# One layer of a post-norm decoder: the rank searches of four heads side by side, selections ahead of them, context in eight parts

## The chip, the cores and the metric

The kernel runs on one core of one Trainium2 chip, as one launch. The metric is device time in microseconds. The kernel before was timed three times: median 5632.22 us (5630.01 to 5635.16). The execution that the profiler recorded is another one, and its own time is 5640.61 us.

## What is computed

A decoder layer over x of shape (4, 1024, 512): windowed self-attention, then a block with cross-attention to a context of shape (4, 2048, 384), then a butterfly feed-forward, each followed by a layer norm. The change touches the cross-attention alone. Of the reference it is this part:

```python
scores = jnp.einsum('bthd,bghd->bhtg', Q, K) / np.sqrt(DH)       # H = 4 heads of 32
scores = jnp.where(vision_mask[:, None, None, :], scores, -jnp.inf)
topv, topi = jax.lax.top_k(scores, K_TOP)                        # 32 of 2048
probs = jax.nn.softmax(topv, axis=-1)
attn = jnp.zeros_like(scores).at[bi, hi, ti, topi].set(probs)
attn_mean = attn.mean(axis=1)                                    # over the heads
c_t = jnp.einsum('btg,bgd->btd', attn_mean, x_vision @ Wv)
```

Every row of every head keeps its 32 largest scores out of 2048; all others get weight zero.

## The kernel before

The layer is a sequence of stages, each with its own buffers and semaphores. `stage_cross` (L1230 to L1641) does the part above up to the mix of the context rows with `attn_mean`. It works on 32 tiles of 128 query rows (`TILES`, L32), eight to a batch (`TPB`, L33). The order of the work is written out by hand, one program for each engine, and the engines meet at semaphores; every engine runs its program in order. Buffers that carry one tile to the next are double (index t % 2).

For tile t and head h:

- **SP** (`_(sp)`) loads the keys of a batch (`keys`), the queries of a tile (`queries`), the parts of the context (`context`, L1317: four parts of 512 rows for a batch through two buffers `raw`, so that parts 2 and 3 wait for `s_clo`), and stores the mixed rows (`store`).
- **PE** computes `scores(t, h)` (L1400: 4 matmuls of 128x512) into `ps_s`, which holds one head: it waits until the head before was copied (`s_sc`). `sum_flags` (L1407) adds the flags of all rows. `turn(t, half, h)` (L1419: 8 matmuls, 16 records) multiplies the selected weights with a diagonal of 1/denominator, so that they come out transposed and summed over the heads. `mix(t)` (L80 to L82: 48 matmuls of 128x384, in three products of high and low parts) multiplies that with the context.
- **ACT** copies scores to `s_buf` (`copy`, L1469), computes the denominators from the 32 tops (`denominators`, L1474), the exponentials of all 2048 scores (`exponentials`, L1480), the high part and a full copy of the turned weights (`hi`, L1487 and L1490), the mixed rows (`mixed`, L1496) and the high part of the context (`context_hi`, L1502).
- **POOL** computes the low parts: `lo` (L1367) of the turned weights, `context_lo` (L1372) of the context.
- **DVE** does the rest. `scan(t, h)` (L1550): 32 MAX8, one for each segment of 64 scores, write 8 ranks of each segment to `cand`. `rank(t, h)` (L1552 to L1571) then finds the 32nd largest: a MAX8 over the low ranks (L1555), four MAX8 over 104 candidates (L1559) with a match_replace between them (L1562, two instructions: the load of the eight values, and the replacement), and a scalar_tensor_tensor with an accumulator that counts candidates at or above the 32nd (L1568, two instructions too). Each reads what the one before wrote, so a `dve.drain()` stands behind each. `settle(t)` (L1573) loads the four flag sums into registers and branches: a head whose sum shows a possible miss is searched over all 2048 scores. `diagonals` (L1602, L1607) and `select(t, h)` (L1596: keep the exponential where the score is at least the 32nd largest) follow.

The order on DVE in iteration t, which does the selections of tile t and the searches of tile t + 1: 8 segments of head 0, the copy of the flag sums (L1616), 8 segments, `settle(t)`, 16 segments, `rank` 0, `diagonals`, `select` 0 and 1, `scan` and `rank` 1, `select` 2 and 3, `scan` and `rank` 2, `scan` and `rank` 3, then L1639 (`nmax`: the negated row maxima) and the semaphore `s_cand`. `sum_flags(t + 1)` on PE waits for `s_cand`, and L1616 of the next iteration for `sum_flags`. `denominators(t)` on ACT waits for `s_chk`, which `settle(t)` gives.

The order on PE in iteration t: `sum_flags(t)`, `mix(t-1)`, `scores(t+1, 2)`, `turn(t, 0, 0..1)`, `scores(t+1, 3)`, `turn(t, 0, 2..3)`, `turn(t, 1, 0)`, `scores(t+2, 0)`, `turn(t, 1, 1..3)`, `scores(t+2, 1)`.

## Time and profile before

| what | value |
|---|---|
| median of 3 runs | 5632.22 us |
| the profiled execution's own time | 5640.61 us |
| its span, first to last instruction | 5638.9 us |
| TensorE clock granted, mean of the span (1.0 is 2.4 GHz) | 0.860 |
| cross-attention stage, in the span | about 1449 to 3059 us |
| PE, DVE, ACT, POOL busy in the whole span | 73%, 56%, 24%, 28% |

Durations below come from the profiled execution. In a timeline the columns are: start in us from the span's start, length in us of the group of instructions on the row, engine, line, operation, out<-in and shapes, number of records (a float32 matmul of `turn` leaves two records), and in brackets the idle time of the engine just before with what ended it. The length of a row with several instructions runs from the first start to the last end.

### The profile page before, as it was taken

The numbers are of one execution on the slowest core, as the hardware profiler recorded it, in microseconds if no ns is written. First come the engines' busy times: TensorE is split into PE (matmuls) and PEld (weight loads), VectorE is DVE, ScalarE is ACT, GpSimd is POOL, SyncE is SP. The second block draws the span as 40 slices with busy tenths as digits, with TensorE's granted clock in tenths as the row PEclk, the third lists the DMA queues.
The fourth block names the chain that finished last, engine by engine and source line by source line (L and its number), as shares of the span: only waits on it lengthen the run. The fifth ranks groups of instructions, "written<-read, shape, count | busy, mean of one in ns | idle before, by whom it ended". The sixth has DMA issues, their size and how long they took to land. (4 is left out here: it accounts for less than half of the span.)

```text
span 5638.9 us, 66043 instructions
## 1 busy us (share of the span) xinstructions
PE 4120.7 (73%) x20932; PEld 3402.2 (60%) x20932; DVE 3146.1 (56%) x9382; ACT 1364.4 (24%) x2042; POOL 1596.3 (28%) x1280
## 2 busy tenths in 40 slices
PE   2331239997467677565676996869699999499998
PEld 1331127775366666465665685657588888388887
DVE  8959933443588888988884454542323433322222
ACT  1210112332344444343442000012211111211111
POOL 2537200000111211110210461320266766133332
PEclk8555669998688888787888998989799999799999
DMA  0025131223301001001000342333412211200000
GB/s 10 17 68 209 45 86 53 82 81 112 121 9 43 21 10 43 17 10 43 21 8 37 117 144 97 112 121 112 128 60 68 76 58 49 90 19 25 20 24 21
DMA packets 238144, 350.47 MB, mean 62 GB/s; under 512 B 67090, under 2 KB 117138, under 8 KB 234002
## 3 DMA queue, kind: packets, MB, share of 16 engines
q1 hardware_dynamic: 145444, 187.77, 10.9%
q10 hardware_dynamic: 89856, 151.04, 7.8%
q0 software_dynamic: 2560, 8.39, 0.4%
q8 instruction: 115, 1.88, 0.1%
q14 instruction: 169, 1.38, 0.1%
HBM read 240.13 MB, written 107.00 MB: 62 GB/s over the span
## 5 line engine op out<-in xcount | busy, mean ns | idle before, releaser
L1419 PE MATMUL xa_ps_t<-xa_diag,xa_s_buf 128*128 128x128 f32 x4096 | 604.0, 316 | 403.8 <-DVE xa_s_buf L1596 331.9
L1419 PEld LDWEIGHTS xa_ps_t<-xa_diag,xa_s_buf 128*128 128x128 f32 x4096 | 581.4, 229 | 442.5 <-DVE xa_s_buf L1596 362.3
L2746 DVE CAST m_act_hl<-m_g 128x512 fp32r<-128x512 f32 x256 | 138.1, 539 | 892.9 <-ACT m_g L2634 892.9
L1550 DVE MAX8 xa_cand<-xa_s_buf 128x8 f32<-128x64 f32 x4096 | 538.6, 216 | 110.9 <-issue 83.3
L2495 POOL TENSOR_TENSOR m_act_hl<-m_g,m_act_hl 128x512 fp32r<-128x512 f32 x256 | 352.7, 1378 | 701.3 <-DVE m_act_hl L2746 701.3
L1367 POOL TENSOR_TENSOR xa_aT<-xa_a,xa_aT 128x512 fp32r<-128x512 f32 x128 | 160.7, 1276 | 1198.5 <-ACT xa_a L1490 1198.5
L2634 ACT ACTIVATE m_g<-m_ps_h,m_b 128x512 f32<-128x512 f32 x256 | 176.1, 688 | 1103.2 <-PE m_ps_h L82 1103.2
L80 PE MATMUL m_ps_h<-m_hT,m_w 128*128 128x512 f32 x1024 | 412.2, 403 | 12.3 <-DVE m_w L2725 7.6
L82 PE MATMUL m_ps_h<-m_hT,m_w 128*128 128x512 f32 x1024 | 404.6, 395 | 0.0
L81 PE MATMUL m_ps_o<-m_w,m_act_hl 128*128 128x512 f32 x1024 | 404.4, 395 | 0.0
L82 PE MATMUL m_ps_o<-m_w,m_act_hl 128*128 128x512 f32 x1024 | 404.4, 395 | 0.0
L81 PE MATMUL m_ps_h<-m_hT,m_w 128*128 128x512 f32 x1024 | 404.3, 395 | 0.0
L80 PE MATMUL m_ps_o<-m_w,m_act_hl 128*128 128x512 f32 x1024 | 404.1, 395 | 0.0
L1469 ACT ACTIVATE xa_s_buf<-xa_ps_s 128x2048 f32<-128x2048 f32 x128 | 241.3, 1885 | 336.1 <-PE xa_ps_s L1400 336.1
L1596 DVE SCALAR_TENSOR_TENSOR xa_s_buf<-xa_s_buf,xa_top,xa_prob 128x2048 f32<-128x2048 f32 x128 | 307.9, 2448 | 6.8 <-ACT xa_prob L1480 0.8
L1480 ACT ACTIVATE xa_prob<-xa_s_buf,xa_nmax 128x2048 f32<-128x2048 f32 x128 | 252.0, 1993 | 15.6 <-DVE xa_s_buf L1596 15.6
L80 PE MATMUL xa_ps_ac<-xa_ctx_hl,xa_aT 128*128 128x384 f32 x512 | 198.8, 388 | 57.0 <-POOL xa_aT L1367 57.0
L80 PEld LDWEIGHTS m_ps_h<-m_hT,m_w 128*128 128x128 f32 x1024 | 193.7, 189 | 60.7 <-issue 10.7
L82 PEld LDWEIGHTS m_ps_h<-m_hT,m_w 128*128 128x128 f32 x1024 | 193.4, 189 | 45.3
L80 PEld LDWEIGHTS m_ps_o<-m_w,m_act_hl 128*128 128x128 f32 x1024 | 192.2, 188 | 46.8 <-POOL m_act_hl L2495 1.0
L82 PEld LDWEIGHTS m_ps_o<-m_w,m_act_hl 128*128 128x128 f32 x1024 | 192.0, 188 | 46.4
L81 PEld LDWEIGHTS m_ps_o<-m_w,m_act_hl 128*128 128x128 f32 x1024 | 192.0, 188 | 45.8
(372 smaller groups left out, 8765.2 us busy)
## 6 DMA issues: line engine op xcount, KB each, us to landing
at_xk<-in_x_dram SPq DMA_DIRECT2D x128, 128.0 KB, 2.6
spectrum<-df_yo ACTq DMA_DIRECT2D x32, 512.0 KB, 2.8
id_raw<-spectrum SPq DMA_DIRECT2D x32, 512.0 KB, 3.9
m_xt<-x ACTq DMA_DIRECT2D x64, 256.0 KB, 3.3
bf_w_dn<-_L_ffn_down_weights_dram SPq DMA_DIRECT2D x7, 2048.0 KB, 7.2
bf_w_up<-in_L_ffn_up_weights_dram ACTq DMA_DIRECT2D x7, 2048.0 KB, 10.1
ky_raw<-in_ctx_dram SPq DMA_DIRECT2D x16, 768.0 KB, 6.4
xa_ks<-kt SPq DMA_DIRECT2D x48, 256.0 KB
```

The lines of the kernel that those rows point to most:

```text
L80: pe.matmul(out, w_hi, m_lo, start=start, stop=False)
L81: pe.matmul(out, w_lo, m_hi, start=False, stop=False)
L82: return pe.matmul(out, w_hi, m_hi, start=False, stop=stop)
L1367: pool.tensor_tensor(aT[:, 1, 4 * g:4 * g + 4, :], a32[:, g % 2, :, :], aT[:, 0, 4 * g:4 * g + 4, :].bitcast(F32), ALU.subtract).then_inc( ...
L1419: last = pe.matmul(ps_t[:, c // 4, c % 4, :], s_buf[:, t % 2, h, k0:k0 + P], diag[:, h, :], start=(h == 0 and c % 4 == 0), stop=(h == HEAD ...
L1469: act.activation(s_buf[:, t % 2, h, :], ps_s[:, :, :].rearrange("p c n -> p (c n)"), ACT.Copy).then_inc(s_sc, 1)
L1480: act.activation(prob[:, h % 2, :], s_buf[:, t % 2, h, :], ACT.Exp, bias=nmax[:, t % 2, h:h + 1], scale=SCALE).then_inc(s_exp, 1)
L1550: dve.max(out=ranks[:, :, g], in_=s_buf[:, t % 2, h, g * SEG:(g + 1) * SEG])
L1596: dve.scalar_tensor_tensor(out=s_buf[:, t % 2, h, :], in0=s_buf[:, t % 2, h, :], scalar=top[:, t % 2, h, TOPK - 1:TOPK], in1=prob[:, h % 2 ...
L2495: pool.tensor_tensor(lo, g32[:, :], hi.bitcast(F32), ALU.subtract).then_inc(s_gl, 1)
L2634: act.activation(g32[:, :], ps_h[:, n % 2, :], ACT.Gelu, bias=b1[:, n:n + 1]).then_inc(s_g, 1)
L2746: dve.tensor_copy(act_hl[:, n % 2, 0, :], g32[:, :]).then_inc(s_gh, 1)
```

## The change

The searches of the four heads of a tile are done together: each of the four heads has its own `cand` and `cand_b`, and every step of `rank` is issued for the four heads in turn, with one drain behind the four. All of it stands at the end of the iteration, behind `scan` 3; `select` 2 and 3 stand ahead of `scan` 3. The flag sums are copied after 16 segments where it was 8, and `settle` comes after all 32. On PE `scores(t+1, 1)` and `scores(t+1, 2)` stand between `sum_flags(t)` and `mix(t-1)`. On ACT and POOL `hi` and `lo` of quarters 2 and 3 of a tile move into the next iteration, on ACT behind `copy(t+1, 1)`. `copy(t+1, 3)` moves behind `exponentials(t, 3)` and `mixed(t-1)`. The context comes in eight parts of 256 rows for a batch, again through two buffers. The output of L1568 that nobody reads goes to `cand_b` as bfloat16, where it went to a buffer of its own.

```diff
 ident = sb("ident", [P, P])
-raw = sb("raw", [P, 2, 4, DV])
+raw = sb("raw", [P, 2, 2, DV])
 ctx_hl = sb("ctx_hl", [P, 2, GC, DV], F32R)
 ...
-cand = sb("cand", [P, 2 * BACK])
-cand_b = sb("cand_b", [P, NW])
+cand = sb("cand", [P, HEADS, 2 * BACK])
+cand_b = sb("cand_b", [P, HEADS, NW])
 top = sb("top", [P, 2, HEADS, TOPK])
-f_junk = sb("f_junk", [P, 2, NW])
 f_weight = sb("f_weight", [P, 2, NW])
 ...
         def context(b, g):
-            i = 4 * b + g
+            i = 8 * b + g
             if i >= 2:
 ...
             sp.dma_start(raw[:, g % 2, :, :],
-                         A["ctx_768"][b][g * 512:(g + 1) * 512, :].rearrange("(n p) v -> p n v", p=P)
+                         A["ctx_768"][b][g * 256:(g + 1) * 256, :].rearrange("(n p) v -> p n v", p=P)
                          ).then_inc(s_raw[g % 2], 16)
 ...
         def store(t):
 ...
             if t % TPB == 0:
-                context(b, 2)
-                context(b, 3)
+                for g in range(2, 8):
+                    context(b, g)
             if t >= 1:
 ...
         def context_lo(b, g):
-            pool.wait_ge(s_chi, 4 * b + g + 1)
-            pool.tensor_tensor(ctx_hl[:, 1, 4 * g:4 * g + 4, :], raw[:, g % 2, :, :],
-                               ctx_hl[:, 0, 4 * g:4 * g + 4, :].bitcast(F32), ALU.subtract).then_inc(s_clo, 1)
+            pool.wait_ge(s_chi, 8 * b + g + 1)
+            pool.tensor_tensor(ctx_hl[:, 1, 2 * g:2 * g + 2, :], raw[:, g % 2, :, :],
+                               ctx_hl[:, 0, 2 * g:2 * g + 2, :].bitcast(F32), ALU.subtract).then_inc(s_clo, 1)
 ...
         for t in range(TILES):
+            if t >= 1:
+                lo(t - 1, 2)
+                lo(t - 1, 3)
             if t % TPB == 0:
-                context_lo(t // TPB, 0)
-                context_lo(t // TPB, 1)
+                for g in range(4):
+                    context_lo(t // TPB, g)
             lo(t, 0)
 ...
             if t % TPB == 0:
-                context_lo(t // TPB, 2)
-                context_lo(t // TPB, 3)
-            lo(t, 2)
-            lo(t, 3)
+                for g in range(4, 8):
+                    context_lo(t // TPB, g)
+        lo(TILES - 1, 2)
+        lo(TILES - 1, 3)
 ...
     def _(pe):
 ...
         def mix(t):
 ...
             if t % TPB == 0:
-                pe.wait_ge(s_clo, 4 * (t // TPB + 1))
+                pe.wait_ge(s_clo, 8 * (t // TPB + 1))
             if t >= 1:
 ...
-        scores(0, 0)
-        scores(0, 1)
-        scores(0, 2)
-        scores(0, 3)
+        for h in range(HEADS):
+            scores(0, h)
         scores(1, 0)
-        scores(1, 1)
         for t in range(TILES):
             sum_flags(t)
+            if t + 1 < TILES:
+                scores(t + 1, 1)
+                scores(t + 1, 2)
             if t >= 1:
                 mix(t - 1)
-            if t + 1 < TILES:
-                scores(t + 1, 2)
             turn(t, 0, 0)
 ...
             turn(t, 0, 3)
-            turn(t, 1, 0)
             if t + 2 < TILES:
                 scores(t + 2, 0)
-            turn(t, 1, 1)
-            turn(t, 1, 2)
-            turn(t, 1, 3)
-            if t + 2 < TILES:
-                scores(t + 2, 1)
+            for h in range(HEADS):
+                turn(t, 1, h)
         mix(TILES - 1)
 ...
         def context_hi(b, g):
-            act.wait_ge(s_raw[g % 2], 16 * (2 * b + g // 2 + 1))
+            act.wait_ge(s_raw[g % 2], 16 * (4 * b + g // 2 + 1))
             if b >= 1:
                 act.wait_ge(s_ac, b * TPB)
-            act.activation(ctx_hl[:, 0, 4 * g:4 * g + 4, :], raw[:, g % 2, :, :], ACT.Copy).then_inc(s_chi, 1)
+            act.activation(ctx_hl[:, 0, 2 * g:2 * g + 2, :], raw[:, g % 2, :, :], ACT.Copy).then_inc(s_chi, 1)
 ...
         for t in range(TILES):
 ...
                 copy(t + 1, 1)
+            if t >= 1:
+                hi(t - 1, 2)
+                hi(t - 1, 3)
             denominators(t)
 ...
             exponentials(t, 2)
-            if t + 1 < TILES:
-                copy(t + 1, 3)
             exponentials(t, 3)
 ...
                 mixed(t - 1)
+            if t + 1 < TILES:
+                copy(t + 1, 3)
             if t % TPB == 0:
-                context_hi(t // TPB, 0)
-                context_hi(t // TPB, 1)
+                for g in range(4):
+                    context_hi(t // TPB, g)
             hi(t, 0)
 ...
             if t % TPB == 0:
-                context_hi(t // TPB, 2)
-                context_hi(t // TPB, 3)
-            hi(t, 2)
-            hi(t, 3)
+                for g in range(4, 8):
+                    context_hi(t // TPB, g)
+        hi(TILES - 1, 2)
+        hi(TILES - 1, 3)
         mixed(TILES - 1)
 ...
     def _(dve):
-        dve.memset(cand[:, :], 0.0)
+        dve.memset(cand[:, :, :], 0.0)
         dve.memset(f_weight[:, 0, :], 1.0)
 ...
         dve.drain()
-        ranks = cand[:, 8:NC].rearrange("p (r g) -> p r g", g=SEGS)
+        ranks = [cand[:, h, 8:NC].rearrange("p (r g) -> p r g", g=SEGS) for h in range(HEADS)]
+        junk = cand_b[:, :, :].rearrange("p h n -> p (h n)").bitcast(BF16).rearrange("p (h a x) -> p h a x", h=HEADS, a=2)
 ...
         def scan(t, h, first, last):
 ...
             for g in range(first, last):
-                dve.max(out=ranks[:, :, g], in_=s_buf[:, t % 2, h, g * SEG:(g + 1) * SEG])
-        def rank(t, h):
+                dve.max(out=ranks[h][:, :, g], in_=s_buf[:, t % 2, h, g * SEG:(g + 1) * SEG])
+        def rank(t):
             k = t % 2
             dve.drain()
-            dve.max(out=cand[:, 0:8], in_=cand[:, NW:NC])
-            dve.drain()
-            src = cand[:, 0:NW]
+            for h in range(HEADS):
+                dve.max(out=cand[:, h, 0:8], in_=cand[:, h, NW:NC])
+            dve.drain()
+            src = cand[:, :, 0:NW]
             for r in range(TOPK // 8):
-                dve.max(out=top[:, k, h, 8 * r:8 * r + 8], in_=src)
+                for h in range(HEADS):
+                    dve.max(out=top[:, k, h, 8 * r:8 * r + 8], in_=src[:, h, :])
                 dve.drain()
                 if r < TOPK // 8 - 1:
-                    dve.match_replace(out=cand_b[:, :], in_to_replace=top[:, k, h, 8 * r:8 * r + 8], in_values=src,
-                                      imm_value=TAKEN)
+                    for h in range(HEADS):
+                        dve.match_replace(out=cand_b[:, h, :], in_to_replace=top[:, k, h, 8 * r:8 * r + 8],
+                                          in_values=src[:, h, :], imm_value=TAKEN)
                     dve.drain()
-                src = cand_b[:, :]
-            dve.scalar_tensor_tensor(out=f_junk[:, :, :], in0=cand[:, :].rearrange("p (a x) -> p a x", a=2)[:, :, 0:NW],
-                                     scalar=top[:, k, h, TOPK - 1:TOPK], in1=f_weight[:, :, :],
-                                     op0=ALU.is_ge, op1=ALU.mult, accum_out=flag[:, k, h:h + 1])
-            dve.drain()
+                src = cand_b[:, :, :]
+            for h in range(HEADS):
+                dve.scalar_tensor_tensor(out=junk[:, h, :, :],
+                                         in0=cand[:, h, :].rearrange("p (a x) -> p a x", a=2)[:, :, 0:NW],
+                                         scalar=top[:, k, h, TOPK - 1:TOPK], in1=f_weight[:, :, :],
+                                         op0=ALU.is_ge, op1=ALU.mult, accum_out=flag[:, k, h:h + 1])
+            dve.tensor_scalar(nmax[:, k, :], top[:, k, :, 0], -SCALE, None, ALU.mult)
+            dve.drain().then_inc(s_cand, 1)
 ...
         def settle(t):
 ...
             if more:
-                scan(t + 1, 0, 0, 8)
+                scan(t + 1, 0, 0, 16)
             if t >= 0:
 ...
             if more:
-                scan(t + 1, 0, 8, 16)
+                scan(t + 1, 0, 16, SEGS)
             if t >= 0:
 ...
             if more:
-                scan(t + 1, 0, 16, SEGS)
-                rank(t + 1, 0)
+                scan(t + 1, 1, 0, SEGS)
             if t >= 0:
 ...
             if more:
-                scan(t + 1, 1, 0, SEGS)
-                rank(t + 1, 1)
+                scan(t + 1, 2, 0, SEGS)
             if t >= 0:
 ...
             if more:
-                for h in range(2, HEADS):
-                    scan(t + 1, h, 0, SEGS)
-                    rank(t + 1, h)
-                dve.tensor_scalar(nmax[:, (t + 1) % 2, :], top[:, (t + 1) % 2, :, 0], -SCALE, None, ALU.mult)
-                dve.drain().then_inc(s_cand, 1)
+                scan(t + 1, 3, 0, SEGS)
+                rank(t + 1)
 st.clear()
 ...
```

## Rows read from the trace of the kernel before

**Rows 1.** Window from first to last L1639: us, busy of PE, PEld, DVE, ACT, POOL; clock

```profile
1500.00:3012.00 1512.00, 1010.97 (x5958) 945.82 (x5958) 1311.98 (x5964) 664.17 (x788) 221.87 (x140) 0.83 0.08 22
```

**Rows 2.** Groups of DVE instructions by line, 1440 to 3065 us: busy, mean ns | idle before

```profile
L1550 DVE MAX8 xa_cand<-xa_s_buf 128x8 f32<-128x64 f32 x4096 | 538.6, 216 | 110.9 <-issue 83.3 <-ACT xa_s_buf L1469 19.2
...
L1596 DVE SCALAR_TENSOR_TENSOR xa_s_buf<-xa_s_buf,xa_top,xa_prob 128x2048 f32<-128x2048 f32 x128 | 307.9, 2448 | 6.8 <-ACT xa_prob L1480 0.8
...
L1568 DVE SCALAR_TENSOR_TENSOR xa_f_junk<-xa_cand,xa_top,xa_f_weight 128x208 f32<-128x208 f32 x128 | 71.5, 559 | 9.9 <-issue 0.4
...
L1639 DVE TENSOR_SCALAR xa_nmax<-xa_top 128x4 f32<-128x4 f32 x32 | 28.5, 892 | 2.6
```

**Rows 3.** Timeline of DVE, one head's scan and rank, up to the next scan

```profile
1955.18 4.15 DVE L1550 MAX8 xa_cand<-xa_s_buf 128x8 f32<-128x64 f32 x32
1959.41 0.33 DVE L1555 MAX8 xa_cand<-xa_cand 128x8 f32<-128x160 f32 x1
1959.81 0.27 DVE L1559 MAX8 xa_top<-xa_cand 128x8 f32<-128x104 f32 x1
1960.15 0.09 DVE L1562 MATCH_VALUE_LOAD xa_cand_b<-xa_top,xa_cand 128x8 f32 x1
1960.23 0.25 DVE L1562 MATCH_REPLACE8 xa_cand_b<-xa_top,xa_cand 128x104 f32<-128x104 f32 x1
1960.56 0.27 DVE L1559 MAX8 xa_top<-xa_cand_b 128x8 f32<-128x104 f32 x1
...
1962.39 0.43 DVE L1568 SCALAR_TENSOR_TENSOR xa_f_junk<-xa_cand,xa_top,xa_f_weight 128x208 f32<-128x208 f32 x1
1962.76 0.08 DVE L1568 DVE_READ_ACCUMULATOR xa_f_junk<-xa_cand,xa_top,xa_f_weight 128x1 f32 x1
1962.91 4.16 DVE L1550 MAX8 xa_cand<-xa_s_buf 128x8 f32<-128x64 f32 x32
```

**Rows 4.** Timeline of DVE, one whole tile, from one L1639 to the next

```profile
2017.08 0.17 DVE L1639 TENSOR_SCALAR xa_nmax<-xa_top 128x4 f32<-128x4 f32 x1
...
2022.73 2.13 DVE L1550 MAX8 xa_cand<-xa_s_buf 128x8 f32<-128x64 f32 x16 [2.77 <-issue]
...
2028.43 0.18 DVE L1602 RECIPROCAL xa_rec<-xa_den 128x4 f32<-128x4 f32 x1
...
2029.68 4.62 DVE L1596 SCALAR_TENSOR_TENSOR xa_s_buf<-xa_s_buf,xa_top,xa_prob 128x2048 f32<-128x2048 f32 x2
...
2061.97 0.17 DVE L1639 TENSOR_SCALAR xa_nmax<-xa_top 128x4 f32<-128x4 f32 x1
```

**Rows 5.** Timelines of ACT: the copy of head 3 before tile 0, a `hi`

```profile
1479.33 1.88 ACT L1469 ACTIVATE xa_s_buf<-xa_ps_s 128x2048 f32<-128x2048 f32 x1 [2.23 <-PE xa_ps_s L1400]
...
2017.57 0.60 ACT L1487 ACTIVATE xa_aT<-xa_ps_t 128x512 fp32r<-128x512 f32 x1 [3.48 <-PE xa_ps_t L1419]
```

**Rows 6.** Timeline of POOL, the two `lo` that `mix` waits for

```profile
2018.73 2.49 POOL L1367 TENSOR_TENSOR xa_aT<-xa_a,xa_aT 128x512 fp32r<-128x512 f32 x2 [9.70 <-ACT xa_a L1490]
```

**Rows 7.** Timelines of PE: `scores` at either clock, `turn` at either clock

```profile
1500.22 2.08 PE L1400 MATMUL xa_ps_s<-xa_ks,xa_qs 128*128 128x512 f32 x4
...
2007.59 3.65 PE L1419 MATMUL xa_ps_t<-xa_diag,xa_s_buf 128*128 128x128 f32 x16 [2.25 <-ACT xa_a L1490]
...
2031.27 1.09 PE L1400 MATMUL xa_ps_s<-xa_ks,xa_qs 128*128 128x512 f32 x4
...
2055.26 5.52 PE L1419 MATMUL xa_ps_t<-xa_diag,xa_s_buf 128*128 128x128 f32 x48
```

**Rows 8.** The context: instructions on `xa_raw` (ns min/median/max), DMA issues (us to landing)

```profile
L1502 ACT ACTIVATE xa_ctx_hl<-xa_raw x16: 1472/1476/1482, 1525.8 to 2731.1; 128x1536 fp32r<-128x1536 f32 x16
L1372 POOL TENSOR_TENSOR xa_ctx_hl<-xa_raw,xa_ctx_hl x16: 3469/3562/5498, 1527.4 to 2734.7; 128x1536 fp32r<-128x1536 f32 x16
...
xa_raw<-in_ctx_dram SPq DMA_DIRECT2D x16, 768.0 KB, 5.6
...
m_xt<-w SPq DMA_DIRECT2D x32, 256.0 KB, 3.5
```

## The prediction, made before the changed kernel ran

> **What bounds the kernel now.** The busy shares of the page come first: over the whole span no engine is above 73%, so a stage has to be chosen. The window of the tile loop [rows 1] is that choice: from the first L1639 to the last are 1512 us for 31 tiles, 48.8 us a tile. DVE is busy for 1312 of them, PE for 1011 at a granted clock of 0.83, ACT for 664. The waits view gives DVE almost nothing but "issue" waits, that is, no other engine keeps it (the largest are the 83.3 us ahead of L1550 [rows 2], one gap a tile). So DVE's own instruction stream sets the time. The timeline of one tile [rows 4] shows it whole: 44.89 us from one L1639 to the next, one gap of 2.77 us (the four flag sums go into registers and `settle` branches), all else back to back. That is a clean tile. The others are longer for two reasons. Heads are searched again in full in two tiles, which stays. And three kinds of DVE instruction are at times stretched [rows 2]: L1639 takes 892 ns in the mean against 170 undisturbed [rows 4], L1568 559 against 430 [rows 3], L1596 2448 against about 2350 (the pair in [rows 4] less its overlap). My reading of the timelines is that this happens where a POOL tensor_tensor runs beside them, as `lo` does behind L1639 [rows 6]. Together: 32 x 0.72 + 128 x 0.13 + 128 x 0.10 = 52 us.
>
> **Part 1, the searches side by side.** One head costs 7.72 us from scan to scan [rows 3]: 4.23 us to the first instruction of `rank`, 3.50 us for `rank`. In `rank` each instruction is followed by a drain, start to start: L1555 0.40 us, L1559 0.34, the L1562 pair 0.41, the L1568 pair 0.52. What does an instruction cost when the next one belongs to another head and needs no drain? 32 scans run in 4.15 us and last 0.216 each [rows 2, 3], so they start every (4.15 - 0.216) / 31 = 0.127 us: each starts 0.09 before its predecessor ends. The accumulator read starts 0.37 after L1568, which lasts 0.43: an overlap of 0.06 to 0.07 between two instructions of different kinds. I price accordingly:
> - L1555: 3 x (0.33 - 0.09) + 0.40 = 1.12 us for four heads.
> - L1559, four rounds: 4 x (3 x 0.18 + 0.34) = 3.52.
> - L1562, three rounds: the load takes 0.08 to the replacement, which gives 0.18 after its overlap with the next head's load (the nearest row is the accumulator read's, of another kind too): 3 x (3 x 0.26 + 0.41) = 3.57. Bounds: 0.24 with 0.09 of overlap, 0.34 with none, so 3.4 to 4.3.
> - L1568: 3 x 0.44 + 0.52 = 1.84.
>
> Sum 10.05 against 4 x 3.50 = 14.0: 3.95 saved. Three scans also lose the drain behind them and flow on: 3 x (4.23 - 32 x 0.127) = 0.5. So 4.45 us a tile, 31 tiles: **-138 us**. The bfloat16 target of L1568 changes nothing: its two inputs stay float32. I take it at zero.
>
> The rule against this part is in the Trainium skill, VectorE: DVE Perf Modes, The DRAIN you can't avoid: after every Vector instruction the pipe empties before the next starts, chaining does not help, only fewer instructions do. By it the change would save explicit drains alone; the starts of the scans every 0.127 us speak against it here.
>
> **Part 2, the first search** (before tile 0) saves less. The copies come every 4.1 us whatever DVE does; the copy of head 3 ends at 1481.2 [rows 5]. Then 4.23 + 10.05 + 0.3 gives 1495.8, where the loop now begins at about 1500.1 (the first row of [rows 7] starts there): **-4.3**.
>
> **Part 3, a clean tile laid out anew.** Let D be the end of L1639 with its drain; all in us after D. DVE: 32 scans of head 0 with the flag copy between them 4.3, register gap 2.8: 7.1. Scan 1: 11.2. Diagonals 1.25 [rows 4]: 12.5. Two selects 4.53 (2029.68 to 2034.21): 17.0. Scan 2: 21.1. Selects 2 and 3: 25.6. Scan 3 29.8, `rank` 39.9, L1639 40.2. (44.89 - 4.45 gives 40.4.) The gap could shrink by the eight more scans that now stand between flag copy and loads, 1.0 us a tile or -31 us, if they queue up behind the loads; or not at all. The nearest row is the gap itself, with eight scans ahead of it, so I take no gain and keep -31 for the range.
>
> Do the others keep up?
> - PE: `sum_flags`, then `scores(t+1, 1)`, with the copy 2.1 behind its start at half clock [rows 7]. ACT: copy until 4.1, `hi` 2 and 3 until 6.0. POOL's `lo` start 1.16 after their `hi` and take 2.5 [rows 5, 6]: 7.7. Only then can `mix(t-1)` start; now it starts at about 1. Its length: 2018.73 + 2.49 to 2031.27 [rows 6, 7], 10.05 us: it ends at 17.8. This is the new wait of the change, and behind it on PE stand all turns and `scores(t+1, 3)`.
> - Turns 0 and 1, 5.27 / 3 = 1.76 each at full clock [rows 7]: 21.3. `scores(t+1, 3)` 22.4, its copy by ACT 1.9: 24.4. DVE wants it at 25.6. **Slack 1.2 us, the smallest in the tile.**
> - Turns 2 and 3 wait for selects: 27.4; `scores(t+2, 0)` 28.5; `hi` 0 and 1: 29.6; four turns: 36.6. The flags are asked for at 40.2. Slack 3.6.
> - ACT has the exponentials of heads 0, 1, 2, 3 by 10.5, 12.5, 17 and 19, each before its select. `copy(t+1, 2)` by 14.4.
>
> So in a clean tile no wait shows, and the moved steps cost nothing as long as this holds.
>
> **Part 4, POOL beside DVE.** `lo` 2 and 3 now run at 5.2 to 7.7, beside scans and the gap; `lo` 0 and 1 at 29 to 31.3, beside scan 3 and the first MAX8 of `rank`. None of the three kinds that are stretched is near. Of the 52 us I keep 4 for context tiles: **-48**.
>
> **Part 5, the context** (4 tiles). Half a part costs 0.74 on ACT and 1.78 on POOL [rows 8]; its load, between 3.5 us (256 KB) and 5.6 (768 KB) for 384 KB: 4.0. Two buffers hold two parts, but ACT now wants four in a row. Parts 0 and 1 are copied by 25.9; part 2 can load only after POOL has done part 0 (27.0) and lands at 31.0, part 3 at 32.8; `hi` 0 and 1 end at 35.5, turns of half 1 begin 6 late after 7 us of idle, so the first at half clock (3.65 [rows 7]): done at 44.7. The flag copy wants PE at 42.5: 2.3 lost. Parts 6 and 7 again wait for loads, ACT is free at 50.0, `copy(t+2, 1)` ends at 51.9 where DVE wants it at 49.9: 2.0 lost. `mix` starts late at 55.6, and with it the copy for scan 3 comes 1.9 late. Sum 6.2 x 4: **+25 us**. Bounds: 0 (each load inside its cover) to 12 a tile, +48.
>
> **Sum** against the profiled execution: 5640.6 - 138 - 4.3 - 48 + 25 = 5475. The median of the runs was 8.4 us under it: **5467 us**.
>
> **Rivals.**
> - *No overlap between heads*: the next instruction starts only when the last has ended. Each instruction gives only its drain: 3 x 0.09 + 12 x 0.09 + 9 x 0.08 + 3 x 0.07 = 2.3 us less a tile, 32 times: 5467 + 73 = 5540. For it: L1562's load may have to wait until the replacement is done with its eight values. Against: the scans. 10%. It is also what the rule of the Trainium skill named in part 1 would give.
> - *The copy for scan 3 is late.* The slack of 1.2 us goes if `mix` ramps up longer or the two turns behind it run at half clock (3.5 more). At 1 to 2 us a tile, 31 to 62 us: 5498 to 5529. For it: every stall in the chain above adds up here. 17%.
> - *The same part, more of it*, with 3 to 5 us a tile: 5560 to 5620. 6%.
> - *Slower than before*: PE becomes the bound at 1.2 GHz. It idles three times ahead of `mix`, and gaps of that size are followed by half clock now (the row of [rows 7] with 2.25 before it). Its work from 7.7 on is mix 10.05 + turns 14.1 + scores 2.2 = 26.3 us; if all of it takes twice as long, PE ends at 63 and not 36.6, and a tile takes about 60 us: 31 x 20 more, 6080. It decides from the point where PE's work takes 9 us more (45.7 a tile, the 165 us given back), a third more than reckoned. Against: from `mix` to the last turn PE is idle for hardly 2 us. 4%.
> - *The change does not do what it says* (another thing than the stream of DVE sets the time, and nothing moves): [rows 4] leave no room. 2%.
>
> **How the numbers follow.** The forecast, 5435 to 5498, has 61%. The range takes in the early register loads (-31), the dearer L1562 (+25), the dearer context, the late copy and the case of no overlap: 5435 to 5545. The bound for "same" is 0.2%, 11 us, about what a measurement can tell. Faster has all of the forecast and the first three rivals: 0.93; same 0.02; slower 0.05.
>
> **What would show it.** In the changed profile: L1639 to L1639 in 40.4 us; L1559 starting every 0.18 us within four; L1562 pairs every 0.26; L1639 at 0.17 us always; `mix` starting 7.7 us after L1639; no wait of DVE on an ACT copy except behind context tiles. DVE waiting for `xa_s_buf` in every tile would make it wrong; so would L1562 at 0.34 or PE waited for by the flag copy.

## The result, and the profile after

The changed kernel takes 5427.84 us in the median of 4 runs (5423.54 to 5428.57), the kernel before 5631.78 us (four runs, where the table ahead of the prediction has three): a ratio of 0.9636 (95% interval 0.9619 to 0.9652), 204 us faster. The forecast was 5467 us, with a range from 5435 to 5545. The direction was right; the gain was larger than the range allowed, by 7 us at its low end.

The profiled executions are 217 us apart (5640.61 and 5423.54 us). Where that lies is read from the rows of L1639 before and of L1576 after, which are the same instruction (it writes `nmax` and ends the search). The timeline of DVE, first and last of the 32, with the first scan of the stage; first the kernel before:

```profile
1468.92 4.16 DVE L1550 MAX8 xa_cand<-xa_s_buf 128x8 f32<-128x64 f32 x32 [19.25 <-ACT xa_s_buf L1469]
...
1499.84 0.17 DVE L1639 TENSOR_SCALAR xa_nmax<-xa_top 128x4 f32<-128x4 f32 x1
...
3011.78 1.05 DVE L1639 TENSOR_SCALAR xa_nmax<-xa_top 128x4 f32<-128x4 f32 x1
```

and the changed kernel:

```profile
1461.17 16.47 DVE L1550 MAX8 xa_cand<-xa_s_buf 128x8 f32<-128x64 f32 x128 [17.89 <-ACT xa_s_buf L1465]
1486.95 0.17 DVE L1576 TENSOR_SCALAR xa_nmax<-xa_top 128x4 f32<-128x4 f32 x1
...
2796.22 0.16 DVE L1576 TENSOR_SCALAR xa_nmax<-xa_top 128x4 f32<-128x4 f32 x1
```

| stretch, us | before | after | difference | forecast |
|---|---|---|---|---|
| up to the first scan (see below) | 1468.92 | 1461.17 | -7.8 | 0 |
| first search | 30.92 | 25.78 | -5.1 | -4.3 |
| 31 tiles | 1511.9 | 1309.3 | -202.7 | -161 |
| from there to the end | 2627.1 | 2625.7 | -1.4 | 0 |

Nearly all of it is the loop. The 7.8 us ahead of the first scan are no effect that the runs show: of what stands there the change touches one memset (0.33 us before, 1.12 after) and the size of the context's loads, which are issued behind the keys; and in the traces of the ten variants below, which share the changed kernel's opening, the first scan starts anywhere from 1461.4 to 1469.0 us. A clean tile takes 38.71 us (of the 31 intervals, 17 lie between 38.6 and 38.8) where it took 44.89 [rows 4] and was forecast at 40.4. This is one, in the timeline of DVE of the changed kernel:

```profile
2010.29 0.17 DVE L1576 TENSOR_SCALAR xa_nmax<-xa_top 128x4 f32<-128x4 f32 x1
2010.57 2.13 DVE L1550 MAX8 xa_cand<-xa_s_buf 128x8 f32<-128x64 f32 x16
2012.61 0.13 DVE L1622 CAST xa_flag_i<-xa_ps_f 1x4 int32<-1x4 f32 x1
2012.82 2.13 DVE L1550 MAX8 xa_cand<-xa_s_buf 128x8 f32<-128x64 f32 x16
2017.13 4.15 DVE L1550 MAX8 xa_cand<-xa_s_buf 128x8 f32<-128x64 f32 x32 [2.18 <-issue]
2021.20 0.16 DVE L1608 RECIPROCAL xa_rec<-xa_den 128x4 f32<-128x4 f32 x1
...
2035.55 4.15 DVE L1550 MAX8 xa_cand<-xa_s_buf 128x8 f32<-128x64 f32 x32
2039.77 1.01 DVE L1556 MAX8 xa_cand<-xa_cand 128x8 f32<-128x160 f32 x4
2040.85 0.77 DVE L1561 MAX8 xa_top<-xa_cand 128x8 f32<-128x104 f32 x4
2041.70 0.09 DVE L1565 MATCH_VALUE_LOAD xa_cand_b<-xa_top,xa_cand 128x8 f32 x1
2041.78 0.25 DVE L1565 MATCH_REPLACE8 xa_cand_b<-xa_top,xa_cand 128x104 f32<-128x104 f32 x1
2041.94 0.08 DVE L1565 MATCH_VALUE_LOAD xa_cand_b<-xa_top,xa_cand 128x8 f32 x1
...
2048.28 0.43 DVE L1572 SCALAR_TENSOR_TENSOR xa_cand_b<-xa_cand,xa_top,xa_f_weight 128x208 bf16<-128x208 f32 x1
2048.64 0.09 DVE L1572 DVE_READ_ACCUMULATOR xa_cand_b<-xa_cand,xa_top,xa_f_weight 128x1 f32 x1
2048.64 0.43 DVE L1572 SCALAR_TENSOR_TENSOR xa_cand_b<-xa_cand,xa_top,xa_f_weight 128x208 bf16<-128x208 f32 x1
...
2048.99 0.17 DVE L1576 TENSOR_SCALAR xa_nmax<-xa_top 128x4 f32<-128x4 f32 x1
```

Four heads' searches take from 2039.77 to 2048.99, 9.22 us, where one took 3.50 [rows 3]. The replacement that lasts 0.25 is followed by the next head's value load 0.16 after its start. The accumulator read and the next head's L1572 start at the same time, so a pair costs 0.36. Behind the fourth L1572 L1576 follows at the same pace: this last step has no drain between its instructions and L1576, though the change is described above as one drain behind every step of four. The register gap is 2.18 us where it was 2.77. Apart from that gap there is no wait.

The groups of DVE (columns as in [rows 2]) show the other half of the gain: nothing is stretched any more, but for L1572, which is at 450 against an undisturbed 430.

```profile
L1602 DVE SCALAR_TENSOR_TENSOR xa_s_buf<-xa_s_buf,xa_top,xa_prob 128x2048 f32<-128x2048 f32 x128 | 294.7, 2345 | 4.4 <-ACT xa_prob L1476 0.8
...
L1572 DVE SCALAR_TENSOR_TENSOR xa_cand_b<-xa_cand,xa_top,xa_f_weight 128x208 bf16<-128x208 f32 x128 | 50.5, 450 | 2.4
...
L1576 DVE TENSOR_SCALAR xa_nmax<-xa_top 128x4 f32<-128x4 f32 x32 | 5.3, 166 | 0.0
```

Record by record the traces tie this to POOL. Of the 32 L1639 of the kernel before, the 21 that a POOL instruction overlaps in time take 1270 ns in the mean, the other 11 take 170. Of the 128 L1568 it is 34 at 904 ns against 94 at 434, of the 128 L1596 8 at 3942 against 120 at 2348. The MAX8 of the scans take 216 ns either way. What these three kinds take above their undisturbed length sums to 52 us in the loop of the kernel before and to 3 us in that of the changed one.

Of these 3 us 2 lie in the last interval, which is longer by 2.4 (41.11 us). There is no next tile, so ACT and POOL come to quarters 2 and 3 early, and two of the last four L1572 run beside POOL and take 1.43 and 1.42 us. DVE first, then POOL, in the timelines of the changed kernel:

```profile
2793.50 1.43 DVE L1572 SCALAR_TENSOR_TENSOR xa_cand_b<-xa_cand,xa_top,xa_f_weight 128x208 bf16<-128x208 f32 x1
...
2794.86 1.42 DVE L1572 SCALAR_TENSOR_TENSOR xa_cand_b<-xa_cand,xa_top,xa_f_weight 128x208 bf16<-128x208 f32 x1
...
2793.42 2.63 POOL L1366 TENSOR_TENSOR xa_aT<-xa_a,xa_aT 128x512 fp32r<-128x512 f32 x2 [7.13 <-ACT xa_a L1486]
```

The first of them starts 0.08 us after POOL's first instruction and ends at 2794.93; the second starts 0.07 us before that and ends at 2796.28, when POOL's second has ended at 2796.05. The Trainium skill says of this (SBUF — State Buffer, SBUF: two separate sides) that VectorE and GpSimd share a pair of ports as an exclusive lock, which whoever starts first keeps for the whole instruction, and that a two-port mode or two SBUF inputs are enough to need it. These rows agree: 1.43 where 0.43 is undisturbed, and MAX8, with one input, is not stretched beside POOL. L1639 has only one tensor input and is stretched all the same; whether it runs in such a mode, no row here shows.

Against that stands the context. Around a context tile two intervals together take 9 to 10 us more than two clean ones (38.99 + 48.53 around tile 8). The waits of DVE from 1840 to 1900 us (who waited for whom: us in total, times, longest):

```profile
DVE xa_cand L1550 <- ACT xa_s_buf L1465: 9.1, 3, 4.0
DVE xa_flag_i L1622 <- PE xa_ps_f L1409: 2.5, 1, 2.5
```

### The profile page after: what moved, and what is told of

It is laid out like the page before. It is cut to its first block and busy times, and to the rows that moved or that the text cites. A ratio compares the mean times of both kernels' runs of the same rounds, so it can differ in the third digit from the quotient of the medians.

```text
span 5421.9 us, 65111 instructions
## 1 busy us (share of the span) xinstructions
PE 4071.0 (75%) x20932; PEld 3333.7 (61%) x20932; DVE 2998.4 (55%) x9382; ACT 1368.5 (25%) x2058; POOL 1589.7 (29%) x1296
## 5 line engine op out<-in xcount | busy, mean ns | idle before, releaser
L1421 PE MATMUL xa_ps_t<-xa_diag,xa_s_buf 128*128 128x128 f32 x4096 | 504.5, 284 | 164.6 <-DVE xa_s_buf L1602 98.4
L1421 PEld LDWEIGHTS xa_ps_t<-xa_diag,xa_s_buf 128*128 128x128 f32 x4096 | 487.3, 198 | 196.1 <-DVE xa_s_buf L1602 117.1
L1602 DVE SCALAR_TENSOR_TENSOR xa_s_buf<-xa_s_buf,xa_top,xa_prob 128x2048 f32<-128x2048 f32 x128 | 294.7, 2345 | 4.4 <-ACT xa_prob L1476 0.8
L1402 PE MATMUL xa_ps_s<-xa_ks,xa_qs 128*128 128x512 f32 x512 | 188.7, 501 | 107.1 <-ACT xa_s_buf L1465 85.1
L80 PEld LDWEIGHTS m_ps_o<-m_w,m_act_hl 128*128 128x128 f32 x1024 | 192.5, 188 | 46.6 <-POOL m_act_hl L2496 1.1
L82 PEld LDWEIGHTS m_ps_o<-m_w,m_act_hl 128*128 128x128 f32 x1024 | 192.4, 188 | 46.2
## 6 DMA issues: line engine op xcount, KB each, us to landing
bf_w_up<-in_L_ffn_up_weights_dram ACTq DMA_DIRECT2D x7, 2048.0 KB, 10.1
```

Of the source, the lines that this page charges most:

```text
L80: pe.matmul(out, w_hi, m_lo, start=start, stop=False)
L82: return pe.matmul(out, w_hi, m_hi, start=False, stop=stop)
L1402: last = pe.matmul(ps_s[:, c, :], qs[:, t % 2, h, :], ks[:, h, c * 512:(c + 1) * 512], start=True, stop=True)
L1421: last = pe.matmul(ps_t[:, c // 4, c % 4, :], s_buf[:, t % 2, h, k0:k0 + P], diag[:, h, :], start=(h == 0 and c % 4 == 0), stop=(h == HEAD ...
L1602: dve.scalar_tensor_tensor(out=s_buf[:, t % 2, h, :], in0=s_buf[:, t % 2, h, :], scalar=top[:, t % 2, h, TOPK - 1:TOPK], in1=prob[:, h % 2 ...
```

## The experiments

Ten kernels ran, each timed against the kernel before on the same chip. The kernel before took 5633.64 us on the chip of the first four, 5628.60 on that of the next four and 5638.01 on that of the last two, so a difference of a few us between two kernels is read from their traces and not from the medians. "Tile" is the most frequent interval between two of the `nmax` instructions, read from the timeline.

**A drain behind every instruction of the search.** Order and heads stay as in the changed kernel:

```diff
 for h in range(HEADS):
     dve.max(out=cand[:, h, 0:8], in_=cand[:, h, NW:NC])
-dve.drain()
+    dve.drain()
```

and likewise behind L1561, L1565 and L1572.

> The changed kernel with a drain behind every instruction of the rank search, order kept. Theory (the overlap of one head's instruction with the next one's is what pays): a rank step costs again what it cost alone, 4 x 0.40 + 16 x 0.34 + 12 x 0.41 + 4 x 0.52 = 14.0 us for four heads against 9.2 in the changed kernel, the clean tile goes from 38.7 to 43.5 us, the kernel to 5428 + 32 x 4.8 = 5582 us. Rival (only the 27 drains themselves cost, 0.08 us each, nothing overlaps): tile 40.9 us, kernel 5495 us.

Measured: 5569.95 us, ratio 0.9888 (0.9872 to 0.9905); tiles of 43.5 to 44.4 us. The edit adds 28 drains a tile and not 27, since the step of L1572 had none. The search takes 2196.55 to 2210.56 = 14.0 us again, and each L1572 pair 0.52:

```profile
2208.99 0.44 DVE L1572 SCALAR_TENSOR_TENSOR xa_cand_b<-xa_cand,xa_top,xa_f_weight 128x208 bf16<-128x208 f32 x1
2209.36 0.08 DVE L1572 DVE_READ_ACCUMULATOR xa_cand_b<-xa_cand,xa_top,xa_f_weight 128x1 f32 x1
2209.51 0.43 DVE L1572 SCALAR_TENSOR_TENSOR xa_cand_b<-xa_cand,xa_top,xa_f_weight 128x208 bf16<-128x208 f32 x1
```

So 142 of the 204 us hang on the instructions of different heads running into one another without a drain. The order alone brings nothing in the search. That the kernel came out 12 us under the 5582 has a cause outside the search: in the longer tile the other engines have more slack, and the context tiles cost 14 us over clean ones where they cost 38 in the changed kernel. The rival is out: it forecast 5495. The Trainium skill (VectorE: DVE Perf Modes, The DRAIN you can't avoid) says that the next instruction does not start until the pipe is empty, and in the same paragraph that one which is not held starts earlier. The prediction took only the first sentence from it. The changed kernel's rows agree with the second: without a drain the starts come 0.07 to 0.09 us before the predecessor's end, for the replacement and the accumulator's instruction too.

**`hi` and `lo` of quarters 2 and 3 back in their own iteration** (ACT and POOL; the same edit in both):

```diff
-                    if t >= 1:
-                        lo(t - 1, 2)
-                        lo(t - 1, 3)
...
+                    lo(t, 2)
+                    lo(t, 3)
```

> The changed kernel with hi and lo of quarters 2 and 3 back in their own iteration, on ACT and POOL alone. Theory (POOL beside L1572 and L1576 stretches them): lo then runs at about 38 to 40.5 us after the last L1576, just where L1572 and L1576 of the search stand; their means rise by some 0.3 us and more, a tile takes 1 to 2 us more, the kernel 5460 to 5490 us. Rival (the place of lo does not matter): 5428 us, L1572 at 0.43 and L1576 at 0.17 us.

Measured: 5454.27 us, ratio 0.968 (0.9664 to 0.9696). Tiles of 38.7, 39.8 and 40.8 us side by side. The groups show where it went:

```profile
L1566 DVE SCALAR_TENSOR_TENSOR xa_cand_b<-xa_cand,xa_top,xa_f_weight 128x208 bf16<-128x208 f32 x128 | 66.1, 571 | 2.4
...
L1570 DVE TENSOR_SCALAR xa_nmax<-xa_top 128x4 f32<-128x4 f32 x32 | 17.8, 556 | 0.0
```

571 and 556 ns where the changed kernel has 450 and 166 (line numbers are six lower here). 128 x 0.12 + 32 x 0.39 + 128 x 0.02 for the selections = 31 us; the medians differ by 26. The theory holds, at 6 us under its band. As in the kernel before, the stretched records are those that POOL overlaps: the 35 such L1566 take 944 ns in the mean, the other 93 take 431; the 12 such L1570 take 1215, the other 20 take 161. Intervals are 38.7 as in the changed kernel, or longer by 1.1 or 2.1 us, according to which instructions meet POOL.

**The flag copy after 24, and after 8, of the 32 segments** (two kernels):

```diff
-                        scan(t + 1, 0, 0, 16)
+                        scan(t + 1, 0, 0, 24)
...
-                        scan(t + 1, 0, 16, SEGS)
+                        scan(t + 1, 0, 24, SEGS)
```

> The changed kernel with the flag copy after 24 segments, so 8 scans stand between it and the register loads, as in the kernel before. Theory (the gap is the 3.6 us from the first load to the next scan, less the scans already queued; the loads start once about ten scans are still to run): gap 2.8 us and not 2.2, tile 39.3, kernel 5446 us. Rival (the gap does not depend on it): 5428 us.

> The changed kernel with the flag copy after 8 segments, so 24 scans stand between it and the register loads. Theory (a queue takes only about ten scans ahead of the loads): gap 2.2 us as with 16, tile 38.7, kernel 5428 us. Rival (all scans run ahead of the loads, eight more hide 1.0 us more): gap 1.2 us, tile 37.7, kernel 5397 us.

Measured: 5445.16 us (0.9666, 0.965 to 0.9683), tile 39.3, and 5427.85 us (0.9636, 0.962 to 0.9652), tile 38.7. The next scan in either, from the timelines:

```profile
2066.95 4.16 DVE L1550 MAX8 xa_cand<-xa_s_buf 128x8 f32<-128x64 f32 x32 [2.76 <-issue]
```

```profile
2059.98 4.16 DVE L1550 MAX8 xa_cand<-xa_s_buf 128x8 f32<-128x64 f32 x32 [2.17 <-issue]
```

With eight scans behind the flag copy the gap is 2.76 us, with 16 it is 2.18, with 24 it stays 2.17. The rows of the register loads say why: the first starts 0.2 us after the scans resume with 8 behind, 0.6 with 16, 1.7 with 24. With 16 and with 24 that leaves 11 scans still to start in most tiles (9 in a few). DVE's sequencer gets that far ahead and no farther. From the first load to the next scan are 3.7 us in most tiles of all three (four loads with the tests of their bounds, then four branches), so about 1.5 us can be hidden behind scans, the rest not. The Trainium skill gives VectorE a queue of eight (Advanced Engine Details and Errata, Engine Queue Depths); what is measured here is that and mostly three more.

**DVE's part and the context's alone**, with the orders of PE, ACT and POOL as before:

```diff
-                    if t + 1 < TILES:
-                        scores(t + 1, 1)
-                        scores(t + 1, 2)
                     if t >= 1:
                         mix(t - 1)
+                    if t + 1 < TILES:
+                        scores(t + 1, 2)
...
+                    if t + 2 < TILES:
+                        scores(t + 2, 1)
```

(and `hi`, `lo`, `turn(t, 1, 0)` and `copy(t+1, 3)` at their old places).

> The changed kernel with the orders of PE, ACT and POOL as before (hi and lo in their own iteration, scores(t+1, 1) at the end of the iteration before, mix ahead of scores(t+1, 2), copy(t+1, 3) ahead of exponentials(t, 3)); DVE and the eight context parts as changed. Theory: DVE's part gives most, but select 3 waits for its exponential by about 0.5 us, and lo stretches L1572 and L1576: tile about 41 us, kernel 5480 to 5520 us. Rival (the other engines' orders do not matter): 5428 us.

Measured: 5511.80 us, ratio 0.9793 (0.9773 to 0.9813), tile 41.0 us. The size was right, the reason was not. L1569, which is L1572 of the changed kernel, is at 432 ns, undisturbed: in that order the search falls between POOL's instructions (in the tile below POOL works until 2040.80 and again from 2050.48, L1569 runs from 2045.86 to 2047.36). The tile is longer by waits of scan 2 for its copy and of the flag copy for PE:

```profile
2050.38 0.15 DVE L1619 CAST xa_flag_i<-xa_ps_f 1x4 int32<-1x4 f32 x1 [0.68 <-PE xa_ps_f L1406]
...
2066.14 4.16 DVE L1547 MAX8 xa_cand<-xa_s_buf 128x8 f32<-128x64 f32 x32 [1.30 <-ACT xa_s_buf L1465]
```

Scan 2 starts 18.57 us after the tile's first scan (2047.57), where the changed kernel has 16.41 (2010.57 to 2026.98): these two waits are nearly all of the 2.3 us. So of the 204 us about 120 come with the other engines in their old order (the context's eight parts apart); their new order is worth the other 84. Both waits end at PE: the flag sums stand behind `scores(t+2, 1)`, and `scores(t+1, 2)` behind `mix`. No run changed PE's order alone. Context tiles suffer most here (53 to 54 us): they make 14 of the 84.

**The context's parts spread over four places; then with three buffers as well:**

```diff
                     if t % TPB == 0:
-                        for g in range(4):
-                            context_hi(t // TPB, g)
+                        context_hi(t // TPB, 0)
+                        context_hi(t // TPB, 1)
                     hi(t, 0)
                     hi(t, 1)
+                    if t % TPB == 0:
+                        context_hi(t // TPB, 2)
+                        context_hi(t // TPB, 3)
```

with parts 4 and 5 behind `copy(t+2, 0)`, and 6 and 7 behind `hi(t, 3)` in the next iteration; POOL likewise. For three buffers: `raw` is `[P, 3, 2, DV]`, a part goes to buffer i % 3 and waits for `s_clo >= i - 2`.

> The changed kernel with the eight context parts taken two by two at four places (ahead of hi 0 and 1, behind them, behind copy(t+2, 0), behind hi 2 and 3 of the next iteration) where it took four in a row twice. Theory (a third part in a row waits on ACT for a load, and DVE waits for ACT's copies): the 9.1 us that a context tile takes more go to 3 to 5 us, kernel 5408 to 5415 us; no wait of ACT for the context's DMA above 1 us. Rival (the work itself, not the wait for the loads, costs the time): 5428 us.

> As the run with the context parts spread, and with three buffers for the parts where it had two. Theory: no load is waited for; a context tile takes 0 to 3 us more than a clean one, kernel 5396 to 5408 us. Rival (the loads were covered already with two): as the spread version.

Measured: 5417.42 us (0.9625, 0.9608 to 0.9643) and 5405.92 us (0.9603, 0.9585 to 0.962). The two intervals around tile 8 take 42.4 + 42.5 us and 40.2 + 41.9, against 39.0 + 48.5: 10.1 us over two clean ones, 7.5 and 4.7. The intervals of the ratios overlap with that of the changed kernel; the loop of 31 tiles in the traces, 1309.3 us in the changed kernel, 1299.8 and 1288.6 in these two, shows the gain. ACT's wait for the context's DMA in the three kernels:

```profile
ACT xa_ctx_hl L1498 <- DMA xa_raw<-in_ctx_dram: 49.4, 16, 5.4
```

```profile
ACT xa_ctx_hl L1501 <- DMA xa_raw<-in_ctx_dram: 18.3, 16, 2.2
```

```profile
ACT xa_ctx_hl L1503 <- DMA xa_raw<-in_ctx_dram: 7.1, 4, 1.9
```

Spreading alone took 10 us off the kernel, not 13 to 20, since waits of 0.6 to 2.2 us for loads were left; and with three buffers one load a batch is still waited for, against the theory. With three buffers the kernel's time is in the band, but a context tile still costs 4.7 and not 0 to 3. Two things remain. In the second interval it is scan 3: `mix` waits for parts 6 and 7, and the copy behind it comes 3.3 us late with two buffers, 2.7 with three (around tile 8). In the first it is POOL again: spread out, `context_lo` now meets the instructions that count candidates (L1583 here), which take 3.1 of the 3.7 us with two buffers and all of the 1.5 with three. DVE, then POOL, with three buffers:

```profile
1845.71 1.96 DVE L1583 SCALAR_TENSOR_TENSOR xa_cand_b<-xa_cand,xa_top,xa_f_weight 128x208 bf16<-128x208 f32 x1
...
1845.64 1.80 POOL L1373 TENSOR_TENSOR xa_ctx_hl<-xa_raw,xa_ctx_hl 128x768 fp32r<-128x768 f32 x1 [0.61 <-ACT xa_ctx_hl L1503]
```

**One register load a tile.** The four flags are also summed, and the single ones are loaded only if the sum shows a doubt:

```diff
                         dve.tensor_copy(flag_i[:, 0:HEADS], ps_f[:, :])
+                        dve.tensor_reduce(out=flag_i[:, HEADS:HEADS + 1], in_=ps_f[:, :], axis=AX.X, op=ALU.add)
...
+                    total = dve.value_load(flag_i[0:1, HEADS:HEADS + 1], min_val=0, max_val=P * NW * 16)
+                    with dve.If(total > HEADS * P * TOPK):
```

> The changed kernel with the sum of the four flags as a fifth value: one register load and one branch a tile, the four others only where it shows a doubt. Theory (the register gap is loads and branches, and the copy for scan 3 has 1.0 us of slack): the gap of 2.2 us goes, but scan 3 then waits about 1.2 us for its copy: tile 37.7, kernel 5397 us. Rival (nothing else binds): tile 36.6, kernel 5363 us.

Measured: 5410.68 us, ratio 0.9612 (0.9594 to 0.963), tile 37.8. The gap has gone (the last 16 scans of head 0 and the 32 of head 1 run on as one group of 48), and scan 3 waits:

```profile
2008.63 6.41 DVE L1550 MAX8 xa_cand<-xa_s_buf 128x8 f32<-128x64 f32 x48
...
2030.42 4.16 DVE L1550 MAX8 xa_cand<-xa_s_buf 128x8 f32<-128x64 f32 x32 [1.05 <-ACT xa_s_buf L1465]
```

2.18 less, 1.05 more make 1.13, of which the tile shows 0.94: the slack of the copy for scan 3 was about 1 us, as reckoned. The kernel gained 17 us (the loop 20, from 1309.3 to 1289.2), not the 31 expected, since some tiles wait longer (39.3 to 39.7) and the contexts no less.

**And `scores(t+1, 3)` directly behind `mix(t-1)`:**

```diff
                         mix(t - 1)
+                    if t + 1 < TILES:
+                        scores(t + 1, 3)
                     turn(t, 0, 0)
                     turn(t, 0, 1)
-                    if t + 1 < TILES:
-                        scores(t + 1, 3)
```

> As the run with one register load, and on PE scores(t+1, 3) directly behind mix(t-1), ahead of the turns of heads 0 and 1. Theory (the 1.05 us for which scan 3 waited in that run is PE's order and nothing else): the copy of head 3 is done 3.5 us earlier, no wait is left in a clean tile, tile 36.7 us, kernel 5411 - 31 x 1.1 = 5377 us. Rival (the turns, now 1.1 us later, make the next flags late or scan 3 waits all the same): tile 37.5 us or more, kernel about 5405 us.

Measured: 5369.73 us, ratio 0.953 (0.9514 to 0.9546), tile 36.7: the wait was PE's order, and the turns behind it hold nobody up in a clean tile. The kernel gained 41 us and not 34, since the tiles that had waited longer than 1.05 us lost that too.

**All of these together** (one load, `scores(t+1, 3)` early, parts spread, three buffers):

> One register load, scores(t+1, 3) behind mix, the context parts spread over four places and three buffers for them. Theory: the gains add up, 5428 - 51 (load and order) - 22 (context) = 5355 us; a context tile 2 to 4 us longer than a clean one of 36.7. Rival (with the shorter tile PE or ACT has no slack left for the context, and the context's gain is lost): about 5377 us.

Measured: 5351.57 us, ratio 0.9496 (0.9481 to 0.9512): 76 us below the changed kernel and the fastest version here. Clean tiles take 36.7, around tile 8 it is 38.6 + 39.0; 1.65 of the 1.9 us in the first of these are again instructions stretched beside POOL. Of the scans' waits in DVE's list this is left:

```profile
DVE xa_cand L1561 <- ACT xa_s_buf L1470: 18.2, 2, 18.0
...
DVE xa_cand L1561 <- issue: 4.3, 9, 1.1
```

18.0 of the first row is the wait for the stage's first copy.

## Why the prediction was right or wrong

**What bounds** was right: DVE's own stream, before and after. No other engine is seen in a clean tile, and the forecast waits (`mix` 7.7 us after the search, 6.8 measured; the copy for scan 3 with 1.2 us of slack, 0.9 measured, 2034.64 against 2035.55) are where they were put.

**Part 1, the searches** is the step that failed: the mechanism was right and the price of four heads side by side, 10.05 us, too dear; 9.22 were measured. The mechanism (0.09 us of overlap for each instruction) is shown by the run with the drains put back. Term by term, for four heads: L1555 1.12 forecast, 1.08 measured; L1559 3.52 and 3.40; L1562 3.57 and 3.33, so the lower bound that was left aside (0.24 a pair) was the right one; L1568 1.84 and 1.42. Of these last 0.42 us, 0.25 are that the next head's instruction starts with the accumulator read and not behind it (3 pairs at 0.36 and not 0.44); the other 0.17 are that the prediction took 0.52 for the fourth pair, a drain included, where the change has none: it takes as long as the others. Sum 10.05 and 9.22: 0.83 x 31 = 26 us. The range had room for a dearer search and hardly any for a cheaper one (0.2 us a tile by the lower bound of L1562, or 6 us): for L1568 no bound was given at all. The -31 us of the range's low end were meant for the register gap. With the search at its forecast price the kernel would have come out at about 5454 us, inside.

**The sum used the smaller of two gains.** The tile laid out anew gave 40.2 us, the difference method 40.4, and the difference was not looked into. A clean tile measured 38.71, 1.73 less than 40.44: 0.83 are the search, 0.59 the gap, 0.31 are left. Of these 0.2 stand in the tile of [rows 4] itself. Its flag copy waited for PE, here in the timelines of DVE and PE before:

```profile
2017.37 1.12 DVE L1550 MAX8 xa_cand<-xa_s_buf 128x8 f32<-128x64 f32 x8
2018.61 0.15 DVE L1616 CAST xa_flag_i<-xa_ps_f 1x4 int32<-1x4 f32 x1
...
2018.38 0.19 PE L1407 MATMUL xa_ps_f<-xa_flag,xa_ones 128*1 128x4 f32 x2
```

The copy starts 0.12 us behind the scans and 0.04 behind PE's flag sums, where it starts 0.09 before the scans' end in the changed kernel (2012.61 against 2012.70). The layout had left this out, the difference carried it on. Counted over 31 tiles the 0.31 are 10 us.

**Part 3, the register gap.** "No gain taken, -31 for the range": 0.59 us a tile of 1.0 came, 18 us. The runs with the flag copy moved show why: the sequencer gets ahead by about eleven scans and no more.

**Part 4, POOL beside DVE** was right in place and size: with 44.89 for each of 31 tiles and 70 us for the repeated searches, before has about 50 us left over, and the stretched instructions sum to 52; after, beside the context's 38, 3 are left, 2.4 of them in the last interval. The run with `lo` put back brought half of it back.

**Part 5, the context** had the mechanism and too small a size: 25 us forecast, 38 measured (the eight intervals around the context tiles against 38.71). Around tile 8 the flags waited 2.5 (2.3 forecast), scan 1 4.0 where 2.0 were forecast beyond the gap (4.0 - 2.2 = 1.8), scan 3 3.0 (1.9 forecast); and scan 0, for which nothing was forecast, waited 2.1: `copy(t+2, 0)` stands behind the four parts too.

Together -26 - 18 - 10 + 13 = -41 of the 42 us by which the loop was missed. The context's 13 us too little hid as much of the other errors; that was luck. Outside the loop, 8 of the 52 us between 5475 and 5423.5 lie ahead of the first scan and are scatter, as the openings of the other runs show. Between the medians the miss is 39 us.

**The rivals.** "No overlap" is ruled out by the starts 0.17 us apart. "The copy is late" did not come, though it was 0.9 us away, and the run with one load shows it as soon as the tile shrinks. PE never fell behind: its last turn ended at 2047.4, 1.9 us ahead of the next flags, less than the 3.6 reckoned because DVE got there sooner (PE was done 36.8 us after the search, 36.6 reckoned).

## What to carry to other kernels

Where short dependent VectorE instructions need a drain each, issue several independent chains in turn: here the same instructions took 9.2 us and not 14.0, and of the 4.8 us only 2.2 were the 28 drains (an estimate, at the 0.08 us between an instruction's end and the next start with a drain between). Keep scalar_tensor_tensor with two SBUF inputs, and small instructions like L1639, away from POOL's tensor_tensor in time; here a place beside the MAX8 scans or the register gap cost nothing. When two ways of summing one forecast differ, find out why before taking the smaller, and bound a price from both sides.

## What was not expected

An accumulator read and the next scalar_tensor_tensor start at the same time (2048.64 both). Four register loads with branches cost 3.7 us, of which about 1.5 can be hidden behind queued scans; one load with one branch costs nothing visible in most tiles (gaps of 0.4 to 1.2 us are left in a few). With a drain behind every instruction, gaps of 0.3 to 0.5 us that belong to nothing in the profile ("issue") turn up in about half of the tiles, as they do in the kernel before; in the changed kernel in three. What causes them was not tried. They and waits of scan 2 for its copy, 0.3 to 0.5 us in eight tiles, make up the spread from 43.5 to 44.4 us in that run.
